# Eight resident Toeplitz tiles, one-hot kernel rows and shared statistics in a decoder layer on one core

## The chip, the cores and the metric

The kernel runs on one core of one Trainium2 chip. The metric is the device time of one execution in microseconds, median of several runs.

## What is computed

One pre-norm decoder layer, all in fp32, on x of 4 sequences x 1024 positions x 256 channels:

```
x = x + mixer(layernorm(x))          # a second layernorm (gamma, beta) inside, then a diagonal
                                     # state-space recurrence over the positions, W_out, b_out,
                                     # and the mixer's own residual
x = x + cross_attention(ctx, ctx, layernorm(x))   # 16 heads, 64 keys a sequence
x = x + ffn(layernorm(x))            # 256 -> 1024 gated, two 1024 x 1024 with gelu, -> 256
h = dA * h + dB * u                  # the recurrence, per channel 64 states
y = sum_n C[n] * h[n] + D * u
```

The recurrence is not stepped. The 1024 positions are cut into 16 chunks of 64. For each channel, what a chunk gives to itself is a 64 x 64 lower triangular Toeplitz matrix (row distance 0 to 63, its entries are the channel's kernel row k[m] = sum over n of w[n] exp(-m alpha[n]), with D added at m = 0), and what it receives from earlier chunks goes through the 64 states.

## The kernel before

The layer is one program for five engines, ordered by hand: each engine has a written list of instructions, and semaphores (`wait_ge`, `then_inc`) tie the lists together. It has two parts. The first, roughly the first 104 us, is the mixer (the functions in `mixer_parts`). Then follow a lead-in for the first block of 512 tokens and a loop over eight such blocks for attention and ffn, in which TensorE is almost always busy. The change touches only the mixer and the places that hand over to it.

The mixer works on these tiles. `xres` holds x by tokens, 32 tiles of 128 tokens x 256 channels. `tok` holds x by channels, 64 columns groups of 128 x 128. `GG` holds for every channel the powers from which kernel rows and carried states are made (128 x 8192). `EE` is the exponent table for the states. `TT` is the Toeplitz matrix of 16 channels (times two halves of the partitions): 128 x 1024 a group, eight groups (`NGRP`) in all.

What each engine does there, in its order:

- **VectorE** (`vector`): coefficients; `GG` by six doublings (`double(0)` to `double(5)`, L337), with token statistics (`stats`, L343 and L346) between them; D added into `GG` at row distance 0 (L397); the rest of the statistics; `variances(b)` and `spreads(b)` for tokens' half b = 0 and 1 (L351 to L363), which give the scales and shifts of the double layernorm; `norms(b)` (L370), which applies them to 12 of the 32 column groups of each half (32 less `ACT_SHARE`); the D entries taken out again (L411); then `gamma(n)` and `beta(n)` (L379, L384) on eight parts of `tok`, of which three must be ready before the first octet; then 16 scans over chunks, one for each octet of channels (L431), with the remaining gammas and betas between them.
- **ScalarE** (`scalar`): exponentials; the decay table (L272); `row_evac(v)` four times (L277): two PSUM banks each of kernel rows into `ksb`; `norm_apply(b)` (L284) on `ACT_SHARE` = 20 of the 32 column groups of each half; the exponentials of `EE` (L289); for each octet the output's evacuation (L304), and the residual base (L292).
- **GpSimd** (`gpsimd_prep`, `gpsimd_core`): constants; inverse square roots by `pow` (L240, L244); `mask(e, g)` for g = 0 to 7 (two affine selects each, L211), which clear the upper triangle of a `TT` tile; `values_clear(0)` (L869); 32 bias sums (L216), of which four stand before mask 7 and the rest behind it.
- **TensorE** (`tensor`): kernel rows by 32 matmuls with a block of ones (L461), in four steps v that each fill two banks; each step writes the same sum to 32 partitions of which one is stored; then `state(0, c)`, and a loop over the octets o = 0 to 16: `state(o + 1)` (L470), `within(o)` (L477, reads `TT`) and `carried(o - 1)` (L484). Octet 0 waits for `z_b` 3 (three betas done); even octets wait for `t_mask`.
- **SyncE** (`sync_mixer`, `sync_core`) issues all transfers in program order: inputs, the kernel rows out to memory (8 stores of 4 rows, L175), then back in as overlapping windows, which makes the Toeplitz tiles (`tt_load`, two transfers a group, L141). `TT` is a ring of four tiles (`TT[g % 4]`), so groups 4 to 7 are loaded in `sync_core` after the octets that use groups 0 to 3 (`w_ps`). Then the ffn weights are copied and loaded, once the last state matmuls are done (`h_ps` 16).

Of the kernel before, what the change touches and what calls it, by code (L numbers as in the profile page):

```python
# [25 lines left out]
F32 = mybir.dt.float32  # L26
# [6 lines left out]
P = 128  # L33
# [21 lines left out]
ACT_SHARE = 20  # L55
# [3 lines left out]
def mixer_parts(nc, ctx, a, t):  # L59
# [7 lines left out]
    def sem(name):  # L67
# [12 lines left out]
    ones = sb("ones", [P, 32], "c")  # L80
# [22 lines left out]
    dtc = sb("dtc", [P, 4], "d")  # L103

    TT = [ring[:, 1024 * k:1024 * (k + 1)] for k in range(4)]
    ksb = ring[:, :].rearrange("p (a m) -> p a m", a=8)
# [7 lines left out]
    kps = [[pair[k][:, 512 * h:512 * (h + 1)] for h in range(2)] for k in (2, 0)]  # L114
# [4 lines left out]
    x_in, E_in, xr_in = ([sem(f"m_{n}{g}") for g in range(8)] for n in ("x_in", "E_in", "xr_in"))  # L119
    const, exps, coef, al_st, coef_t, pk_done, g_row, d_add = (  # L120
        sem("m_" + n) for n in ("const", "exps", "coef", "al_st", "coef_t", "pk_done", "g_row", "d_add"))
    k_ps, k_ev, kr_pad, e_rdy, t_mask = (sem("m_" + n) for n in ("k_ps", "k_ev", "kr_pad", "e_rdy", "t_mask"))
    kr_st = sem("m_kr_st")
    T_in = [sem(f"m_T_in{k}") for k in range(4)]
# [14 lines left out]
    def tt_load(e, g):  # L139
        for h in range(2):  # L140
            e.dma_start(TT[g % 4][L * h:L * h + L, :],  # L141
                        bass.AP(t["kr_h"], (8 * h + g) * (GRP * L), [[1, L], [1, GRP * L]])).then_inc(T_in[g % 4], 16)
# [6 lines left out]
    def sync_mixer(e):  # L149
# [18 lines left out]
        e.dma_start(bo[:, :], a["ab"].partition_broadcast(P)).then_inc(wo_in, 16)  # L168
        e.dma_start(woT[:, :, :], a["aW"]).then_inc(wo_in, 16)
        for v in range(4):  # L170
            for h in range(2):
                u = 2 * v + h
                e.wait_ge(k_ev, u + 1)
                c = (1 - h) * (P * L) + v * 2048
                e.dma_start(kr[0, c:c + 2048].rearrange("(q m) -> q m", q=4), ksb[0:P:32, u, :]).then_inc(kr_st, 16)  # L175
        for n in ("xW", "keys", "scl"):
            e.dma_start(t[n], a[n]).then_inc(k_in, 16)
# [4 lines left out]
        for g in range(2, NGRP):  # L182
            entries_load(e, g)

    def sync_core(e):
        for g in range(4, NGRP):
            e.wait_ge(w_ps, 2 * (g - 4) + 2)
            tt_load(e, g)
# [4 lines left out]
        e.wait_ge(w_d, 48)  # L193
        for n in ("w1", "w2", "w3"):
            e.dma_start(t[n].bitcast(F32), t["d" + n]).then_inc(w_in, 16)
# [10 lines left out]
    def mask(e, g):  # L206
        e.wait_ge(T_in[g % 4], 32 * (g // 4 + 1))
# [10 lines left out]
    def gpsimd_prep(e):  # L218
# [27 lines left out]
        for g in range(1, 4):  # L246
            mask(e, g)
# [1293 lines left out]
```

## Time and profile before

| | |
|---|---|
| median of 3 runs | 929.63 us (928.91 to 930.36) |
| the profiled execution's own time | 931.86 us |
| its span in the profile | 929.9 us |
| busy: PE, PEld, DVE, ACT, POOL | 865.2, 703.3, 524.3, 483.3, 183.7 us |
| mean granted TensorE clock | 0.985 of full |
| first octet's matmuls start | 51.24 us |
| last octet's evacuation starts | 103.56 us |

Times in the profile count from the span's start, in microseconds. PE is TensorE's matmuls, PEld its weight loads, DVE is VectorE, ACT ScalarE, POOL GpSimd, and SPq SyncE's queue of transfers. A matmul call in fp32 leaves two matmul records and two weight load records. In a timeline row the first number is the start, the second the time from the start of the first to the end of the last instruction of the row, then engine, line, operation, what is written and read, and the count; in brackets the idle time of the engine ahead of it and what ended it.

### The profile page before, as it was taken

The numbers are of one execution on the slowest core, as the hardware profiler recorded it, in microseconds if no ns is written. First come the engines' busy times: TensorE is split into PE (matmuls) and PEld (weight loads), VectorE is DVE, ScalarE is ACT, GpSimd is POOL, SyncE is SP. The second block draws the span as 40 slices with busy tenths as digits, with TensorE's granted clock in tenths as the row PEclk, the third lists the DMA queues.
The fourth block names the chain that finished last, engine by engine and source line by source line (L and its number), as shares of the span: only waits on it lengthen the run. The fifth ranks groups of instructions, "written<-read, shape, count | busy, mean of one in ns | idle before, by whom it ended". The sixth has DMA issues, their size and how long they took to land.

```text
span 929.9 us, 15452 instructions
## 1 busy us (share of the span) xinstructions
PE 865.2 (93%) x5762; PEld 703.3 (76%) x5762; DVE 524.3 (56%) x943; ACT 483.3 (52%) x745; POOL 183.7 (20%) x201
## 2 busy tenths in 40 slices
PE   1168999899999999999999999999999999999998
PEld 0067867677887778777877787778777887788887
DVE  7996486465556455555655555464655456464422
ACT  2926543566347634754366536753576256734432
POOL 1567710500031002300130005000500040003000
PEclk9689999999999999999999999999999999999999
DMA  9962698500110002000200010001100110001000
GB/s 341 246 169 50 228 386 344 227 1 1 39 58 0 0 23 73 0 0 0 73 22 0 0 62 34 0 0 51 45 0 0 51 45 0 0 23 45 1 1 25
DMA packets 15641, 61.92 MB, mean 67 GB/s; under 512 B 2851, under 2 KB 4646, under 8 KB 14790
## 3 DMA queue, kind: packets, MB, share of 16 engines
q1 hardware_dynamic: 15574, 61.44, 19.2%
q8 instruction: 24, 0.39, 0.2%
q14 instruction: 11, 0.09, 0.0%
q0 software_dynamic: 32, 0.00, 0.0%
HBM read 49.76 MB, written 23.20 MB: 78 GB/s over the span
## 4 chain that ended last, share of the span: by engine, by line
PE 83%; DVE 9%; issue 5%; ACT 2%; DVEq 0%; POOL 0%; DMA 0%; SPq 0%; POOLq 0%
PE pair L1348 44%; PE pair L1335 9%; PE pair L1360 6%; PE pair L1374 4%; PE pair L1277 4%; PE pair L1288 3%; PE pair L1304 3%; PE pair L470 2%; PE pair L477 2%; PE pair L1297 1%; PE pair L1244 1%; PE pair L484 1%; PE pair L539 1%; DVE vbuf L1150 1%; DVE GG L337 1%
## 5 line engine op out<-in xcount | busy, mean ns | idle before, releaser
L952 ACT ACTIVATE vbuf<-pair,scl 128x512 f32<-128x512 f32 x128 | 87.7, 685 | 231.0 <-PE pair L1348 227.8
L1348 PE MATMUL pair<-h2hi,h_turned 128*128 128x512 f32 x512 | 202.7, 396 | 0.0
L1348 PE MATMUL pair<-h2lo,h_turned 128*128 128x512 f32 x512 | 199.5, 390 | 0.0
L1348 PE MATMUL pair<-h1hi,h_turned 128*128 128x512 f32 x384 | 153.4, 399 | 0.0
L1348 PE MATMUL pair<-h1lo,h_turned 128*128 128x512 f32 x384 | 150.1, 391 | 0.0
L1114 DVE TENSOR_TENSOR h1lo<-vbuf,h1hi 128x512 fp32r<-128x512 f32 x80 | 57.7, 722 | 119.5 <-ACT h1hi L953 118.7
L1348 PEld LDWEIGHTS pair<-h2hi,h_turned 128*128 128x128 f32 x512 | 96.1, 188 | 25.2 <-issue 5.9
L1348 PEld LDWEIGHTS pair<-h2lo,h_turned 128*128 128x128 f32 x512 | 96.2, 188 | 19.3
L1114 DVE TENSOR_TENSOR h2lo<-vbuf,h2hi 128x512 fp32r<-128x512 f32 x64 | 44.3, 692 | 107.0 <-ACT h2hi L953 106.7
L1335 PE MATMUL pair<-zThi,w_turned 128*128 128x512 f32 x224 | 91.7, 410 | 4.1 <-DVE vbuf L1150 4.1
L1348 PEld LDWEIGHTS pair<-h1hi,h_turned 128*128 128x128 f32 x384 | 72.1, 188 | 24.7 <-issue 10.5
L1150 DVE SCALAR_TENSOR_TENSOR vbuf<-pair,scl,sg 128x512 f32<-128x512 f32 x64 | 47.9, 749 | 73.7 <-ACT sg L941 57.5
L1335 PE MATMUL pair<-zTlo,w_turned 128*128 128x512 f32 x224 | 88.8, 396 | 0.0
L845 POOL TENSOR_TENSOR lnv<-lnv 128x4 f32<-128x4 f32 x16 | 16.2, 1015 | 345.2 <-DVE lnv L1019 321.5
L941 ACT ACTIVATE sg<-pair,scl 128x512 f32<-128x512 f32 x64 | 44.1, 688 | 77.6 <-PE pair L1335 67.9
L905 ACT ACT_TABLE_LOAD x65 | 83.4, 1283 | 1.1
L1348 PEld LDWEIGHTS pair<-h1lo,h_turned 128*128 128x128 f32 x384 | 72.2, 188 | 14.2
L877 POOL TENSOR_TENSOR h1lo<-vbuf,h1hi 128x512 fp32r<-128x512 f32 x48 | 61.8, 1287 | 76.7 <-ACT h1hi L944 76.7
L470 PE MATMUL pair<-tok,EE 64*64 64x60 f32 x512 | 38.3, 276 | 26.5 <-DVE tok L384 24.9
L1374 PE MATMUL pair<-w_turned,h1hi 128*128 128x256 f32 x256 | 62.8, 285 | 0.0
L1374 PE MATMUL pair<-w_turned,h1lo 128*128 128x256 f32 x256 | 62.3, 283 | 0.0
L1335 PEld LDWEIGHTS pair<-zThi,w_turned 128*128 128x128 f32 x224 | 42.6, 190 | 20.1 <-DVE vbuf L1150 9.4
(143 smaller groups left out, 1584.5 us busy)
## 6 DMA issues: line engine op xcount, KB each, us to landing
h_turned<-d_h SPq DMA_DIRECT2D x2, 4096.0 KB, 15.0
xres<-in_x SPq DMA_DIRECT2D x8, 512.0 KB, 7.4
tok<-in_xs SPq DMA_DIRECT2D x8, 512.0 KB, 12.2
EE<-alpha_rows SPq DMA_DIRECT2D x16, 256.0 KB, 11.0
ring<-kernel_rows SPq DMA_DIRECT2D x16, 256.0 KB, 4.2
xr<-x_rows SPq DMA_DIRECT2D x8, 512.0 KB, 3.5
out<-xr SPq DMA_DIRECT2D x16, 256.0 KB, 2.0
x_rows<-xres SPq DMA_DIRECT2D x7, 512.0 KB, 12.5
```

The lines of the kernel that those rows point to most:

```text
L470: ins = e.matmul(out, EE[L * h:L * h + L, i, :], rhs, start=True, stop=True)
L877: e.tensor_tensor(h1[1][:, m, :], vb[:, m % 2, :], h1[0][:, m, :], ALU.subtract).then_inc(S["lo"], 1)
L905: e.activation(warm[:, 1:2], warm[:, 0:1], function).then_inc(S["warm"], 1)
L941: e.activation(sg[:, m % 2, :], pair[m % 2][:, 0:512], ACT.Silu, scale=sc1[:, m:m + 1]).then_inc(S["sg_rdy"], 1)
L952: e.activation(vb[:, s % 2, :], h_ps[s % 4], ACT.Gelu, scale=sc)
L1114: e.tensor_tensor(dst[1][:, n % HC, :], vb[:, n % 2, :], dst[0][:, n % HC, :], ALU.subtract).then_inc(S["lo"], 1)
L1150: e.scalar_tensor_tensor(vb[:, m % 2, :], pair[m % 2][:, 512:1024], sc2[:, m:m + 1], sg[:, m % 2, :], ALU.mult, ALU.mult).then_inc(S["v_rd ...
L1277: ins = e.matmul(pair[2][:, g * BLK + b * 256:g * BLK + (b + 1) * 256], qa[64 * g:64 * g + 64, h, tile * P:(tile + 1) * P], kblk[64 * g:64 ...
L1335: ins = e.matmul(pair[m % 2][:, 512 * g:512 * g + 512], w[:, k, m * P:(m + 1) * P], zT[part][:, k * BLK:(k + 1) * BLK], start=(k == 0 and ...
L1348: ins = e.matmul(bank, w[:, k, m * P:(m + 1) * P], src[part][:, k, :], start=(k == 0 and part == 0), stop=(k == HC - 1 and part == 1))
L1360: ins = e.matmul(h_ps[m], h1T[:, k, m * P:(m + 1) * P], h1[part][:, k, :], start=(k == 0 and part == 0), stop=(k == HC - 1 and part == 1))
L1374: ins = e.matmul(pair[2][:, m * DM:(m + 1) * DM], h1[part][:, k, m * P:(m + 1) * P], w3T[:, k, :], start=(k == 0 and part == 0), stop=(k = ...
```

## The change

- `TT` has eight tiles: four in `ring`, four in the space of the ffn weights `w1` and `w2`, which are loaded only later. All eight are loaded in `sync_mixer` and none in `sync_core`. `ksb` moves to the space of `w3`.
- Kernel rows: `ones` becomes `pick`, zeros with one column of ones. `pick[:, 3-v:35-v]` puts the sums of step v on partition 32q + v, and the four steps accumulate in the same two banks. So there is one evacuation of two banks in place of four, placed inside `norm_apply(0)` ahead of its column group `ROWS_AT` = 3. The stores stay eight.
- Statistics of the token tiles 8 to 15 (`ACT_STATS`) move from VectorE to ScalarE (`tile_stats`): a Copy and a Square of each tile with accumulated output, and two small activations for every four tiles.
- `ACT_SHARE` goes from 20 to 18, so VectorE normalises 14 column groups of each half.
- The two reads of the D rows move from VectorE to ScalarE (`w_row`), the two adds and the two restores to GpSimd (`d_add`, `g_back`). Three clears on VectorE move to its start. `norms(1)` moves behind `beta(1)`.
- GpSimd makes its small masks ahead of the Toeplitz masks, starts these only at `z_h` 3 (gamma(2) done), makes all eight in one go, and then does all bias sums; `values_clear(0)` follows them.
- TensorE gets five matmuls without use for the result (128 x 512, `ident` by `GG`) after `z_b` 2, ahead of the first states.
- `bo`, `woT`, `xW`, `keys` and `scl` are transferred after the Toeplitz tiles.

```
-ACT_SHARE = 20
+ACT_SHARE = 18
+ACT_STATS = (8, 16)
+ROWS_AT = 3
...
     def sync_mixer(e):
...
-        e.dma_start(bo[:, :], a["ab"].partition_broadcast(P)).then_inc(wo_in, 16)
-        e.dma_start(woT[:, :, :], a["aW"]).then_inc(wo_in, 16)
-        for v in range(4):
-            for h in range(2):
-                u = 2 * v + h
-                e.wait_ge(k_ev, u + 1)
+        for h in range(2):
+            e.wait_ge(k_ev, h + 1)
+            for v in range(4):
...
         for g in range(4):
             tt_load(e, g)
-        for g in range(2, NGRP):
+            if g in (1, 2):
+                entries_load(e, g + 1)
+        for g in range(4, NGRP):
             entries_load(e, g)
+            if g == 6:
+                e.wait_ge(nat_v, 1)
+            tt_load(e, g)
+        e.dma_start(bo[:, :], a["ab"].partition_broadcast(P)).then_inc(wo_in, 16)
...
     def sync_core(e):
-        for g in range(4, NGRP):
-            e.wait_ge(w_ps, 2 * (g - 4) + 2)
-            tt_load(e, g)
...
     def gpsimd_prep(e):
...
+        e.wait_ge(d_in, 32)
+        e.wait_ge(w_row, 2)
+        e.wait_ge(g_row, 7)
+        for row in (0, N):
+            v = GG[row:row + 1, :, L - 1]
+            e.tensor_tensor(v, v, edit[row:row + 1, 0, :], ALU.add).then_inc(d_add, 1)
+        e.wait_ge(d_add, 2)
+        power(0)
+        e.wait_ge(k_ps, 1)
+        e.wait_ge(powd, 1)
+        for row in (0, N):
+            e.tensor_copy(GG[row:row + 1, :, L - 1], edit[row:row + 1, 1, :]).then_inc(g_back, 1)
+        e.wait_ge(g_back, 2)
+        power(1)
...
+    def gpsimd_core(e):
+        e.wait_ge(z_h, 3)
+        for g in range(NGRP):
             mask(e, g)
-    def gpsimd_core(e):
+        e.wait_ge(t_mask, 2 * NGRP)
         e.wait_ge(wo_in, 32)
...
+        for tile in range(TILES):
+            bias(e, tile)
...
     def scalar(e):
...
+        def tile_stats(first, until):
+            here, n = slice(first, until), until - ACT_STATS[0]
+            e.wait_ge(xr_in[first // 4], 16)
+            if n > 4:
+                e.wait_ge(t_var, n - 4)
+            for j in range(first, until):
+                e.activation(junk[j % 4], xres[:, j, :], ACT.Copy, accum_out=tsum[:, 0, j:j + 1]).then_inc(t_sum, 1)
+            e.wait_ge(t_sum, n)
+            e.activation(tsum[:, 1, here], tsum[:, 0, here], ACT.Copy, scale=-1.0 / (16 * DM)).then_inc(t_mean, 1)
+            e.activation(mvn[:, here, 0], tsum[:, 0, here], ACT.Copy, scale=1.0 / DM).then_inc(t_mean, 1)
+            e.wait_ge(t_mean, n // 2)
+            for j in range(first, until):
+                e.activation(junk[j % 4], xres[:, j, :], ACT.Square, bias=tsum[:, 1, j:j + 1], scale=1.0 / 16, accum_out=mvn[:, j, 1:2]).then_inc(t_var, 1)
...
     def vector(e):
+        for k in range(2):
+            e.memset(hps[k], 0.0).then_inc(h_zero, 1)
+        e.memset(dec[:, :, 0], 0.0).then_inc(dec0, 1)
...
-        stats(4, 8)
+        stats(4, ACT_STATS[0])
+        last_two(0)
         double(5)
...
-        stats(8, 16)
         variances(0)
-        stats(16, 26)
+        stats(SB, SB + 8)
         spreads(0)
-        stats(26, 32)
+        stats(SB + 8, TILES)
+        last_two(1)
         variances(1)
...
         gamma(0)
-        norms(1)
         beta(0)
         gamma(1)
         beta(1)
+        norms(1)
         gamma(2)
         beta(2)
...
     def tensor(e):
...
-                    ins = e.matmul(kps[v % 2][h][32 * q:32 * q + 32, :], ones[N * h:N * h + N, 0:32], GGf[N * h:N * h + N, c:c + 8 * L], start=True, stop=True)
-            ins.then_inc(k_ps, 1)
+                    ins = e.matmul(kps[h][32 * q:32 * q + 32, :], pick[N * h:N * h + N, 3 - v:35 - v], GGf[N * h:N * h + N, c:c + 8 * L], start=(v == 0), stop=(v == 3))
+        ins.then_inc(k_ps, 1)
+        e.wait_ge(pk_done, 7)
+        e.wait_ge(w_row, 2)
+        e.wait_ge(z_b, 2)
+        for _ in range(5):
+            e.matmul(pair[3][:, 0:BLK], ident[:, :], GGf[:, 0:BLK], start=True, stop=True)
...
-        values_clear(0)
         m["gpsimd_core"](e)
+        values_clear(0)
```

## Rows read from the trace of the kernel before

**Rows 1.** Timeline of TensorE, the first octet's state matmuls.

```profile
51.24 1.86 PE L470 MATMUL pair<-tok,EE 64*64 64x60 f32 x30 [24.90 <-DVE tok L384]
```

**Rows 2.** Timeline of VectorE, 0 to 60 us.

```profile
6.00 0.58 DVE L332 COPY edit<-pair 1x128 f32<-1x128 f32 x2
...
19.36 0.84 DVE L397 TENSOR_TENSOR GG<-GG,edit 1x128 f32<-1x128 f32 x2
20.23 0.43 DVE L343 BATCH_NORM_STATS2 stn<-xres 128x6 f32<-128x256 f32 x1
...
31.55 1.02 DVE L406 MEMSET pair<- 128x512 f32 x2
32.49 2.98 DVE L370 TENSOR_SCALAR tok<-tok,spread 128x128 f32<-128x128 f32 x12
...
37.42 1.23 DVE L379 TENSOR_TENSOR tok<-tok,gam 128x1024 f32<-128x1024 f32 x1
38.56 4.95 DVE L370 TENSOR_SCALAR tok<-tok,spread 128x128 f32<-128x128 f32 x12
...
44.56 1.21 DVE L379 TENSOR_TENSOR tok<-tok,gam 128x1024 f32<-128x1024 f32 x1
...
49.14 2.04 DVE L384 TENSOR_TENSOR tok<-tok,bet 128x1024 f32<-128x1024 f32 x1
...
53.28 1.36 DVE L431 TENSOR_TENSOR_SCAN scan<-dec,pair 128x128 f32<-128x128 f32 x4
```

**Rows 3.** Timeline of ScalarE, 0 to 95 us.

```profile
7.09 1.80 ACT L272 ACTIVATE dec<-a 128x1920 f32<-128x1920 f32 x1
...
26.44 1.08 ACT L277 ACTIVATE ring<-pair 128x512 f32<-128x512 f32 x2 [0.24 <-PE pair L461]
28.61 7.80 ACT L284 ACTIVATE tok<-tok,spread 128x128 f32<-128x128 f32 x20 [1.09 <-issue]
...
90.45 2.07 ACT L292 ACTIVATE xres<-xres,ngn,rsn 128x256 f32<-128x256 f32 x4
```

**Rows 4.** Timeline of GpSimd, 20 to 110 us.

```profile
23.92 2.93 POOL L240 TENSOR_TENSOR rn<-sv,mhalf 128x16 f32<-128x16 f32 x1 [20.04 <-DVE sv L354]
...
40.95 5.53 POOL L244 TENSOR_TENSOR rsm<-svn,mhalf 128x32 f32<-128x32 f32 x1
46.55 11.05 POOL L211 TENSOR_SCALAR_AFFINE_SELECT ring<-ring 64x1024 f32<-64x1024 f32 x6
...
89.78 17.25 POOL L216 TENSOR_TENSOR xres<-xres,bo 128x256 f32<-128x256 f32 x25
```

**Rows 5.** Groups by line, 0 to 104 us: busy, mean ns, idle before.

```profile
L461 PE MATMUL pair<-GG,ones 64*32 64x512 f32 x64 | 5.7, 848 | 14.9 <-DVE GG L397 14.6 <-ACT ring L277 0.2
```

**Rows 6.** Timeline of SyncE's queue: stores of kernel rows, first Toeplitz loads.

```profile
23.02 5.04 SPq L175 DMA_DIRECT2D kernel_rows<-ring  x8
...
33.65 4.96 SPq L141 DMA_DIRECT2D ring<-kernel_rows  x8
```

**Rows 7.** Stretches: each engine's busy time, granted clock, DMA share, GB/s.

```profile
40.00:50.00 10.00, 0.00 (x0) 0.00 (x0) 9.93 (x16) 7.34 (x16) 9.78 (x4) 0.50 1.03 238
...
54.00:55.00 1.00, 1.00 (x43) 1.00 (x39) 1.00 (x4) 0.00 (x0) 0.87 (x2) 0.57 1.03 238
...
60.00:70.00 10.00, 9.90 (x361) 9.71 (x358) 8.67 (x18) 5.70 (x9) 3.31 (x4) 1.00 0.40 110
```

**Rows 8.** Chain that ended last: a projection's 16 matmul records, 128x256 each.

```profile
106.47 3.72 PE pair L539 x16
```

**Rows 9.** TensorE's waits, 56 to 103 us: total, times, longest.

```profile
PE pair L477 <- issue: 5.2, 4, 3.0
PE pair L470 <- issue: 1.5, 1, 1.5
```

**Rows 10.** Instruction queue's packets, MB, share: 50 to 60 us, then 60 to 100 us.

```profile
q8 instruction: 1, 0.02, 0.8%
...
q8 instruction: 10, 0.16, 1.8%
```

More of the change, by code:

```diff
@@ L113, in mixer_parts @@
     yps = [pair[k][:, 512 * h:512 * (h + 1)] for k in (2, 0) for h in range(2)]
-    kps = [[pair[k][:, 512 * h:512 * (h + 1)] for h in range(2)] for k in (2, 0)]
+    kps = [pair[2][:, 512 * h:512 * (h + 1)] for h in range(2)]
+    junk = [pair[0][:, DM * k:DM * (k + 1)] for k in range(4)]
     ident = t["ident"]
@@ L193, in sync_core @@
         e.wait_ge(w_d, 48)
+        e.wait_ge(w_ps, NOCT)
         for n in ("w1", "w2", "w3"):
@@ L240, in gpsimd_prep @@
             e.tensor_tensor(rn[:, 0, here], sv[:, here], mhalf[:, 0:SB], ALU.pow).then_inc(powd, 1)
-        mask(e, 0)
-        e.wait_ge(t_mask, 2)
+        e.wait_ge(d_in, 32)
[12 more added lines that the diff above has]
+        power(1)
         e.wait_ge(nat_v, 1)
+        e.wait_ge(powd, 2)
         e.tensor_tensor(rsm[:, :], svn[:, :], mhalf[:, :], ALU.pow).then_inc(natural, 1)
         e.wait_ge(natural, 1)
-        for g in range(1, 4):
+    def gpsimd_core(e):
+        e.wait_ge(z_h, 3)
+        for g in range(NGRP):
             mask(e, g)
-        e.wait_ge(t_mask, 8)
-    def gpsimd_core(e):
+        e.wait_ge(t_mask, 2 * NGRP)
         e.wait_ge(wo_in, 32)
-        done = 0
-        for g, until in ((4, 0), (5, 0), (6, 0), (7, 4), (None, TILES)):
-            for tile in range(done, until):
-                bias(e, tile)
-            done = until
-            if g is not None:
-                e.wait_ge(base_b, done)
-                mask(e, g)
-                e.wait_ge(t_mask, 2 * g + 2)
+        for tile in range(TILES):
+            bias(e, tile)
     def scalar(e):
@@ L272, in scalar, with row_evac @@
         e.activation(dec[:, :, 1:CH], a64[:, :].unsqueeze(2).to_broadcast([P, P, CH - 1]), ACT.Copy).then_inc(dec_rdy, 1)
-        def row_evac(v):
-            e.wait_ge(k_ps, v + 1)
+        e.wait_ge(g_row, 1)
+        for row in (0, N):
+            e.activation(edit[row:row + 1, 1, :], GG[row:row + 1, :, L - 1], ACT.Copy).then_inc(w_row, 1)
+        def tile_stats(first, until):
[11 more added lines that the diff above has]
+                e.activation(junk[j % 4], xres[:, j, :], ACT.Square, bias=tsum[:, 1, j:j + 1], scale=1.0 / 16, accum_out=mvn[:, j, 1:2]).then_inc(t_var, 1)
+        def row_evac():
+            e.wait_ge(k_ps, 1)
             for h in range(2):
-                e.activation(ksb[:, 2 * v + h, :], kps[v % 2][h], ACT.Copy).then_inc(k_ev, 1)
+                e.activation(ksb[:, h, :], kps[h], ACT.Copy).then_inc(k_ev, 1)
         def norm_apply(b):
@@ L292, in residual_base @@
             e.activation(xres[:, j, :], xres[:, j, :], ACT.Identity, bias=ngn[:, j:j + 1], scale=rsn[:, j:j + 1]).then_inc(base, 1)
-        for v in range(4):
-            row_evac(v)
-        e.wait_ge(const, 9)
+        for first in range(*ACT_STATS, 4):
+            tile_stats(first, first + 4)
+        e.wait_ge(const, 10)
         norm_apply(0)
-        entry_exp(0)
         norm_apply(1)
-        for g in range(1, 3):
+        for g in range(3):
             entry_exp(g)
@@ L330, in vector @@
         e.tensor_copy(GG[:, :, L - 1:L], wT.unsqueeze(2)).then_inc(g_row, 1)
-        for row in (0, N):
-            e.tensor_copy(edit[row:row + 1, 1, :], wT[row:row + 1, :]).then_inc(d_add, 1)
         def double(k):
@@ L476, in within @@
                 rows = slice(L * h, L * h + L)
[L477 removed]
+                ins = e.matmul(yps[o % 4][rows, c * BC:(c + 1) * BC], TT[o // 2 % 8][rows, (i % GRP) * PAD:(i % GRP) * PAD + L], tok[rows, :, i], start=(c == 0), stop=False)
             return ins
```

95 lines of the change are left out of this document (48 added, 47 removed).

## The prediction

> **What bounds the kernel now.** I read the chain that ended last first, then the timelines of the five engines to 110 us, then stretches of 10 us, then the queues. Behind the mixer the chain is TensorE itself, and nothing there is edited. In the mixer TensorE has almost nothing to do until the first octet: [rows 1] shows it idle for 24.90 us until the third `beta` ends, and starting at 51.24. So the mixer's front is a chain over VectorE and ScalarE, and what the change is worth is how much earlier that third beta and the first scans come. The reader should follow it in [rows 2] and [rows 3]: doublings to 19.2, D adds, statistics, spreads, norms from 28.61 on ScalarE and from 32.49 on VectorE, gamma(0) at 37.42, the second norms 38.56 to 43.5, beta(2) 49.14 to 51.2, first scan done at 54.64. VectorE has no idle time of note in it. In [rows 7] VectorE is busy 9.93 of 10 us in the stretch from 40.
>
> From the first octet on, TensorE sets the pace: [rows 7], second row, has 361 matmul records in 9.90 us, 27.4 ns each, so an octet of 96 records takes 2.6 us. The ring of four Toeplitz tiles does not hold it: TensorE's waits from 56 to 103 us are 5.2 and 1.5 us of "issue" [rows 9], none on a mask. So eight resident tiles by themselves save nothing there; what they give is freedom in placing GpSimd's masks.
>
> **The sum, step by step.** Before-times stand in the rows, after-times are worked out.
>
> 1. The two D reads leave VectorE (0.58 from 6.00), two aggregates (0.2 together) come ahead of `double(5)`: it ended just ahead of the adds at 19.36, at 19.2 [rows 2], so now at 19.2 - 0.5 + 0.2 = 18.9. The three clears that left (two are the 1.02 at 31.55) now lie at VectorE's very start, where it waits for its first inputs, and cost nothing; without that cover about 1.2.
>
> 2. D adds on GpSimd. The trace has no such add there. VectorE's are 0.42 each [rows 2]; above, a 128x256 bias sum on GpSimd is 0.69 (17.25/25) [rows 4]; below I go to 0.2. I take 0.45, as one row of 128 elements is nearer to VectorE's row: done at 19.85, +-0.5.
>
> 3. Kernel rows on TensorE: the same 64 records, busy 5.7 [rows 5], now without waits for evacuations: 19.9 to 25.7.
>
> 4. Statistics on ScalarE. It is free when the decay table is done, 7.09 + 1.80 = 8.9 [rows 3]; two D reads of 0.2 follow. A 128x256 activation with two pointer operands is paced at 0.52 (2.07/4) [rows 3]; 16 of them are 8.3, four small ones at 0.2 and their waits 1.1, so 18.7 without any price for the accumulated output. For that the trace has nothing. Bounds: a gain, since Copy has no pointer operands and may be faster (-2), and a further small activation each (+0.2 each, +3.2). I take +1: done at 19.7. Nothing is queued on ScalarE meanwhile that anyone needs (its row evacuations came from 22.4 on). Who waits is `variances(0)` on VectorE, free at 18.9, and behind it `power(0)` on GpSimd, free at 19.85. So up to 19.8 this is nearly free, then each microsecond counts fully.
>
> 5. `power(0)` 2.93 [rows 4]: 19.9 to 22.8. VectorE makes eight statistics meanwhile (pace 0.39, 20.23 onward [rows 2]), 3.1, also done near 23. Spreads take 1.0, about what ScalarE idled ahead of 28.61 [rows 3]: ready at 23.9, against 28.5 before. 4.6 us gained, from eight tiles fewer (3.1) and ten fewer statistics behind the first `variances`, up to where the pow ends last.
>
> 6. ScalarE: three column groups (0.39 each, 7.80/20), then the evacuation, for which `k_ps` comes at 25.7, ends 26.8 (1.08 for two banks), then 15 groups: 32.6 [rows 3]. Without `k_ps` in time this end moves with it. VectorE: eight statistics 3.1, small ones 0.5: 27.5; 14 norms at 0.244 (2.98 for 12 [rows 2], beside a pow on GpSimd): 30.9. `power(1)`: GpSimd copies D back after 25.7 (0.9), then 27.4 to 30.3, hidden. Spreads(1) until 31.9. The copies and the clear that stood ahead of gamma(0) are gone too. gamma(0) starts at 32.7, bound by ScalarE with 0.8 to spare on VectorE; before 37.42.
>
> 7. Two gammas and two betas at 1.15 (44.56 and its successor [rows 2], beside the long pow): 37.3. `norms(1)`, 14 groups: 3.4 at the undisturbed pace; before, it took 4.9 for 12 because masks began at 38.27 beside it [rows 2]. The bound above is that pace, 5.8. GpSimd now runs only the long pow and tiny masks here: 3.4, to 40.7. ScalarE's second half, 32.6 + 18 x 0.39 = 39.6, is hidden. gamma(2) 1.15: 41.9. Then the masks start, and beta(2) runs beside them: 2.04 as at 49.14: 43.9, against 51.2. gamma(3) likewise: 46.0; first scan 46.0 to 47.3, against 54.64: 7.3 gained.
>
> 8. TensorE. The five useless matmuls are 10 records of 128x512. A 128x256 record is 0.23 at the high clock [rows 8], so 0.47, and 0.93 at the low one. The granted clock is 0.50 (1.2 GHz) over 40 to 50 [rows 7]; in the trace it rose within the stretch 54 to 55 (mean 0.57), some 3.6 us after the first octet began, and is 1.00 at 60. With the same delay from 37.3: four records slow, six fast, 6.5 us, done at 43.8, just as beta(2) ends. Bounds: never fast, 46.6; still under the scan's 47.3 for the states alone, costing about 1. The first octet then runs at 2.4 GHz; before, it ran at 1.2 GHz up to there. Mask 0 is two selects at 1.84 (11.05/6 beside gammas [rows 4]): 45.6, then 64 records, 47.4. So octet 1's carried part starts at about 47.4, against 55.4: 8.0 gained.
>
> 9. Transfers. The row stores start at 26.3 in place of 23.02 and issue for 5.0 [rows 6], to 31.4; before, the last ended at 28.06 and the first load was issued at 33.65, behind a full queue. With `bo`, `woT` and three more moved behind, I expect 2.5 for the last landing: loads from 34, tile 0 at about 38, needed at 41.9. Even the old 5.6 leaves a microsecond or so. Later tiles: 512 KB a group for each of `TT` and `EE` at 238 GB/s [rows 7] is 4.4 us a pair; tile 7 lands near 65. Masks go on at 1.84 a select to about 70, group g done at 45.6 + 3.7g, needed at about 5.7g + 45; in time. `bo` is in by 68, bias sums 70 to 94 at 0.69; before they ended at 107. The ffn weights are triggered by the last states and so shift along.
>
> 10. Inside the loop: while masks run, VectorE's gamma or beta is 2.04 in place of 1.2, with a 1.3 scan 3.35 per octet against TensorE's 2.6. The lag grows 0.6 to 0.7 an octet, has about 1.3 of slack, and TensorE's own stalls give more back: I charge 0.5. And 0.5 for stalls in code fetch beside transfers that now last to 65 and not to 58.
>
> Sum: 8.0 - 0.5 - 0.5 = 7.0. The profiled execution had 931.86 with a span of 929.9, so 924.9 and 922.9; the median of the runs is 2.2 below the former: **922.6 us**. Differences below 0.2% (1.9 us) I count as no change.
>
> **A rule that speaks against it.** In [rows 2] four gammas and betas keep their 1.15 beside GpSimd's 5.53 us pow (40.95 to 46.5 [rows 4]). 
> - *The lock moves into the loop.* If select and gamma alternate worse than 2.04, VectorE becomes the pace for eight octets: 0.75 each less the slack, 8 x 0.75 - 1.3 - 1.5 = 3.2: 925.3. Against: scans beside masks keep 1.36 [rows 2].
> - *Code fetch beside transfers; this is the way to slower.* TensorE's longest stall, 3.0 us [rows 9], came with the only instruction block that its queue (q8) fetched in the stretch with full DMA engines; ten more follow in the 40 us behind 60 [rows 10], mostly with idle DMA engines, and with them only 2.2 + 1.5 us of stalls [rows 9]. After the change, at one block in 4 us from 47 to 65, five or so fall into the full stretch. Each that shows costs up to 3.0: one or two, 925.6; four, 12 us less what overlaps VectorE's lag, about 930 to 932. From three it eats the gain. For: one of one was exposed. Against: its excess over the other stalls is only 1.5. The Trainium skill (Runtime: NRT & Kernel Launch, "Instruction fetch mechanics") calls crossing a block mostly hidden; the 3.0 disagrees.
> - *The long pow does block gammas*: gamma(0) at 35.8, 3.1 lost: 925.7.
> - *Hidden anyway*: something behind the mixer with a time of its own (ffn weights, `keys`) takes up the gain: no change, 929. Against: all of it is triggered by mixer steps that move too.
>
> **Chances.** Forecast 0.65 (own range 920.7 to 924.5: GpSimd's adds +-0.5, accumulation -0 to +1.5, lag 0 to 1, fetch 0 to 1). Dear accumulation 0.12, lock in the loop 0.07, fetch 0.12 (half of it still faster, 0.02 no change, 0.04 slower), pow 0.02, hidden 0.02. Faster 0.65 + 0.12 + 0.07 + 0.06 + 0.02 = 0.92, same 0.04, slower 0.04. The range takes in the three cases near 925 and leaves out the fetch case's tail: 920.7 to 926.3.
>
> **What would show it.** Right: spreads(0) copied near 23; gamma(0) near 32.7; `norms(1)` 3.4 for 14; first states near 44; first scan near 46; granted clock 1.00 there; no wait on masks in the loop; last evacuation near 96.5 and everything behind shifted alike. Wrong: VectorE idle before `variances(0)` on ScalarE's Square; extra instructions after each accumulating one; TensorE "issue" waits in the loop well above 5.2 + 1.5 in total; TensorE waiting for scans; mask 0 waiting for its load.

## The result

The changed kernel takes **932.48 us** (median of 10 executions, 931.24 to 934.33), the kernel before, run beside it, 930.10. The ratio is 1.0024, 95% interval 1.0014 to 1.0033: slower by 0.24%, where 922.6 us was forecast. The profiled execution is 934.33 us, the slowest of the ten, with a span of 932.6, 2.7 us above the span before.

Up to the first scan everything came as forecast. ScalarE's timeline (start, duration, engine, line; the accumulated output shows as an instruction of its own) answers to step 4:

```profile
15.30 0.36 ACT L303 ACTIVATE pair<-xres 128x256 f32<-128x256 f32 x1
15.61 0.18 ACT L303 ACTIVATION_READ_ACCUMULATOR pair<-xres 128x1 f32 x1
...
17.65 0.46 ACT L309 ACTIVATE pair<-xres,tsum 128x256 f32<-128x256 f32 x1
18.05 0.19 ACT L309 ACTIVATION_READ_ACCUMULATOR pair<-xres,tsum 128x1 f32 x1
```

GpSimd's timeline, answering to [rows 4]: D adds, first power, long power, the masks, the last 20 bias sums.

```profile
19.26 1.14 POOL L258 TENSOR_TENSOR GG<-GG,edit 1x128 f32<-1x128 f32 x2 [15.21 <-DVE GG L377]
20.48 2.94 POOL L252 TENSOR_TENSOR rn<-sv,mhalf 128x16 f32<-128x16 f32 x1
...
31.33 5.53 POOL L269 TENSOR_TENSOR rsm<-svn,mhalf 128x32 f32<-128x32 f32 x1
...
42.77 13.40 POOL L221 TENSOR_SCALAR_AFFINE_SELECT ring<-ring 64x1024 f32<-64x1024 f32 x8 [4.22 <-issue]
...
89.17 13.84 POOL L226 TENSOR_TENSOR xres<-xres,bo 128x256 f32<-128x256 f32 x20 [1.86 <-ACT xres L331]
```

VectorE's timeline, answering to [rows 2]: gamma(0), norms(1), gamma(2), beta(2), gamma(3), first scan.

```profile
32.85 1.22 DVE L425 TENSOR_TENSOR tok<-tok,gam 128x1024 f32<-128x1024 f32 x1 [0.17 <-issue]
...
37.65 3.67 DVE L416 TENSOR_SCALAR tok<-tok,spread 128x128 f32<-128x128 f32 x14
41.42 1.23 DVE L425 TENSOR_TENSOR tok<-tok,gam 128x1024 f32<-128x1024 f32 x1
42.69 1.23 DVE L430 TENSOR_TENSOR tok<-tok,bet 128x1024 f32<-128x1024 f32 x1
43.83 2.17 DVE L425 TENSOR_TENSOR tok<-tok,gam 128x1024 f32<-128x1024 f32 x1
45.92 1.34 DVE L466 TENSOR_TENSOR_SCAN scan<-dec,pair 128x128 f32<-128x128 f32 x4
```

The first scan starts at 45.92 (46.0 forecast, 53.28 before): 7.4 us gained. At TensorE it is less. Its first matmul of the carried part (47.4 forecast) stands in its timeline at 49.39:

```profile
49.39 0.32 PE L522 MATMUL pair<-scan,GG 64*64 64x64 f32 x2
```

And in the same view of the kernel before:

```profile
55.41 0.26 PE L484 MATMUL pair<-scan,GG 64*64 64x64 f32 x2
```

That is 6.0 us gained and not 8.0. TensorE's timeline of the changed kernel shows the wait for mask 0 and then three holes:

```profile
47.05 0.30 PE L508 MATMUL pair<-tok,EE 64*64 64x60 f32 x2 [1.23 <-POOL ring L221]
...
52.99 0.27 PE L522 MATMUL pair<-scan,GG 64*64 64x64 f32 x2 [2.43 <-issue]
...
61.81 0.37 PE L515 MATMUL pair<-tok,ring 64*64 64x64 f32 x2 [5.06 <-issue]
...
70.54 0.27 PE L515 MATMUL pair<-tok,ring 64*64 64x64 f32 x1 [4.41 <-issue]
```

"Issue" means that nothing in the trace was waited for; 2.43 + 5.06 + 4.41 = 11.9 us. The stretches, answering to [rows 7] (PE's busy time comes first after the length; then, at the end, the granted clock, DMA share, GB/s):

```profile
50.00:60.00 10.00, 4.32 (x142) 3.91 (x139) 6.43 (x10) 1.64 (x2) 9.07 (x8) 0.94 1.04 229
60.00:70.00 10.00, 4.32 (x127) 4.09 (x127) 5.23 (x10) 3.21 (x5) 6.32 (x6) 0.74 1.04 251
70.00:80.00 10.00, 9.46 (x314) 9.46 (x314) 6.01 (x13) 4.94 (x9) 6.04 (x7) 0.75 0.15 34
```

In 20 us TensorE makes 142 + 127 records, where [rows 7] has 361 in ten. The DMA engines are full up to 70 (shares of 0.87 and 0.40 in these stretches before), and behind each of the two long holes TensorE runs at 1.2 GHz again: stretches of 1 us at 63, 71 and 74 are granted 0.50, the one at 75 is at 0.98. TensorE's instruction blocks come on their own queue, q8; its packets in 50 to 60, 60 to 70 and 70 to 80 us:

```profile
q8 instruction: 2, 0.03, 1.7%
...
q8 instruction: 1, 0.02, 0.9%
...
q8 instruction: 3, 0.05, 2.1%
```

Before, 60 to 70 had three. Narrow windows of the same view give each packet's place: in the changed kernel they start at 50.13, 58.97 and 67.72 (the expectation of the first experiment has these 0.2 us late) and take 1.3 to 1.4 us each, and the three holes end at 52.99, 61.81 and 70.54, each 2.8 to 2.9 us behind the start of its packet. Once under way a block is hardly slower than elsewhere (0.9 to 1.4 us behind 70); what is late is its start. In the kernel before, the 3.0 us hole ends 2.7 us behind the packet of 56.92. A smaller one, 1.5 us, ends 2.45 us behind the packet of 69.81, with a DMA share of only 0.26 from 70 to 80, so not every exposed block had full DMA engines beside it. The evacuation of the last octet, from ScalarE's timeline of the changed kernel:

```profile
104.38 0.60 ACT L342 ACTIVATE tok<-pair 128x512 f32<-128x512 f32 x1 [0.57 <-PE pair L522]
```

And the same view of the kernel before:

```profile
103.56 0.60 ACT L304 ACTIVATE tok<-pair 128x512 f32<-128x512 f32 x1 [0.57 <-PE pair L484]
```

So between the first scan and the last evacuation the 7.4 us are lost, and 0.8 more. Of these 8.2, 5.9 are added waits at issue (12.6 in place of 6.7) and 1.2 the wait for mask 0. The other 1.9 us of the span's 2.7 come behind the mixer, where nothing is edited: in the stretches from 165 to 175 the granted clock is lower than before. The changed kernel's:

```profile
165.00:170.00 5.00, 2.12 (x6) 1.67 (x6) 3.56 (x7) 1.32 (x2) 1.27 (x1) 0.72 0.26 107
170.00:175.00 5.00, 5.00 (x18) 3.96 (x17) 0.75 (x1) 1.47 (x3) 1.28 (x1) 0.60 0.86 315
```

The same stretches of the kernel before:

```profile
165.00:170.00 5.00, 2.87 (x8) 2.24 (x9) 2.74 (x4) 0.63 (x1) 1.28 (x1) 0.75 0.26 105
170.00:175.00 5.00, 5.00 (x26) 4.15 (x25) 1.50 (x2) 2.41 (x4) 2.30 (x2) 0.91 1.09 413
```

### The profile page after: what moved, and what is told of

The parts are those of the page before. It is cut to its first block, busy times and chain, and to the rows that moved or that the text cites. A ratio compares the mean times of both kernels' runs of the same rounds, so it can differ in the third digit from the quotient of the medians.

```text
span 932.6 us, 15491 instructions
## 1 busy us (share of the span) xinstructions
PE 872.9 (94%) x5772; PEld 708.6 (76%) x5772; DVE 519.1 (56%) x925; ACT 487.9 (52%) x773; POOL 186.0 (20%) x206
## 4 chain that ended last, share of the span: by engine, by line
PE 83%; DVE 7%; issue 6%; ACT 2%; POOL 1%; DVEq 0%; DMA 0%; SPq 0%; POOLq 0%
PE pair L1386 44%; PE pair L1373 9%; PE pair L1398 6%; PE pair L1412 4%; PE pair L1315 4%; PE pair L1326 3%; PE pair L1342 3%; PE pair L508 2%; PE pair L515 2%; PE pair L1335 1%; PE pair L1282 1%; PE pair L522 1%; PE pair L577 1%; DVE vbuf L1188 1%; DVE GG L377 1%
## 5 line engine op out<-in xcount | busy, mean ns | idle before, releaser
L1152 DVE TENSOR_TENSOR h2lo<-vbuf,h2hi 128x512 fp32r<-128x512 f32 x64 | 44.2, 691 | 107.0 <-ACT h2hi L991 106.7
L1386 PEld LDWEIGHTS pair<-h1hi,h_turned 128*128 128x128 f32 x384 | 72.1, 188 | 24.7 <-issue 10.5
L897 POOL TENSOR_TENSOR kblk<-keys,hmask 128x256 f32<-128x256 f32 x18 | 10.7, 613 | 208.0 <-PE pair L1315 207.9
```

Of the source, the lines that this page charges most:

```text
L1152: e.tensor_tensor(dst[1][:, n % HC, :], vb[:, n % 2, :], dst[0][:, n % HC, :], ALU.subtract).then_inc(S["lo"], 1)
L1386: ins = e.matmul(bank, w[:, k, m * P:(m + 1) * P], src[part][:, k, :], start=(k == 0 and part == 0), stop=(k == HC - 1 and part == 1))
```

## The experiments

Theory F: with 16 full DMA engines TensorE's next instruction block comes late, and the change brings TensorE into that stretch. Rivals: L, GpSimd's selects and VectorE's operations hold each other up; A, the load on the transfers doesn't matter. Later came theory G: what the mixer gains is given back where the next phase waits for bias sums. All results in one table. "Issue" is TensorE's waits of that kind from 30 to 106 us, "last" the start of the last octet's evacuation, both from the profiled execution. The ratios are to the kernel before on the same chip, whose medians were 930.63 (e1 to e4), 930.23 (e5 to e8), 931.55 (e9 to e11) and 930.62 (e12). Where the text compares two runs in microseconds, these are differences of medians, and the kernel before alone moved by 1.45 from one set to another; the ratios are the safer comparison.

| run | us | ratio, 95% interval | issue | last |
|---|---|---|---|---|
| before | 930.10 | 1 | 6.7 | 103.56 |
| after | 932.48 | 1.0024 (1.0014, 1.0033) | 12.6 | 104.38 |
| e1_late | 930.30 | 0.9999 (0.9988, 1.0010) | 10.2 | 102.22 |
| e2_traffic | 935.27 | 1.0061 (1.0046, 1.0075) | 10.5 | 108.10 |
| e3_wide | 1039.33 | 1.1179 (1.1161, 1.1198) | 0.0 | 203.17 |
| e4_small_masks | 930.72 | 1.0010 (1.0000, 1.0020) | 12.4 | 103.62 |
| e5_paced | 932.24 | 1.0024 (1.0009, 1.0040) | 1.3 | 95.06 |
| e6_fill | 930.23 | 1.0008 (0.9995, 1.0021) | 9.6 | 102.66 |
| e7_fill_paced | 927.11 | 0.9967 (0.9953, 0.9981) | 3.8 | 94.99 |
| e8_fill_late | 928.74 | 0.9983 (0.9971, 0.9994) | 8.6 | 100.97 |
| e9_fill_spread | 924.37 | 0.9930 (0.9912, 0.9949) | 4.3 | 96.54 |
| e10_before_paced | 934.23 | 1.0037 (1.0022, 1.0052) | 0.3 | 107.83 |
| e11_paced_spread | 927.87 | 0.9969 (0.9957, 0.9982) | 3.0 | 97.3 |
| e12_before_eased | 932.48 | 1.0027 (1.0015, 1.0040) | 5.8 | 103.12 |

**Tiles 4 to 7 loaded late**, in the changed kernel:

```diff
     def sync_core(e):
+        for g in range(4, NGRP):
+            e.wait_ge(w_ps, 2 * (g - 4) + 2)
+            if g == 6:
+                e.wait_ge(nat_v, 1)
+            tt_load(e, g)
```

> The changed kernel with its eight tiles, but groups 4 to 7 loaded as in the kernel before: each only after the octets that use group g - 4. Theory F (TensorE's code blocks are fetched late while the queues are full of transfers): in the changed kernel the blocks came 8.8 us apart (50.35, 59.19, 67.95) with the DMA engines full to about 71 us, and 3.6 us apart later. Here 2 MB less are queued, so the full stretch ends near 60: the stall at 66 goes (4.4 us), the one at 57 stays or shrinks; 926 to 929. Rival L (GpSimd's masks beside VectorE's gammas set the octets' pace): masks 0 to 3 are as dense as before, so the time stays within 1 us of the changed kernel, 931.5 to 933.

2.2 us came back, in the last evacuation and in the median alike; the waits at issue fell only from 12.6 to 10.2. The time, 930.30, lies outside both ranges, between them. Fewer transfers in the stretch help, but two holes of the three stay (2.0 and 4.5 us), and the third is down to 1.1. The profiled execution gained more, 5.2 us of span: 3.0 of them behind the mixer, where its clock is granted 1.00 from 165 to 175 (0.72 and 0.60 in the changed kernel).

**Useless loads in the kernel before**, 2 MB behind the exponent groups:

```diff
         for g in range(2, NGRP):
             entries_load(e, g)
+        for g in range(4):
+            for h in range(2):
+                e.dma_start(more[...], ...).then_inc(more_in, 16)
...
```

> The kernel before with eight more transfers of 256 KB each, that nothing needs, queued behind the exponent tables (into space that is free until the ffn weights come). Nothing else changes. Theory F: the full stretch goes from 58.5 to about 67; the blocks that came at 60.7 and 64.4 come about 6 us late each, so TensorE's issue waits grow from 6.7 to 11 to 16 us, and the time from 930 to 934 to 938. Rival L, and the rival that the stalls come from the order of the instructions and not from transfers: no change, 930.

Nothing reads these loads in the mixer, and yet it lost 4.5 us there and 4.6 in the time, as F said; the waits at issue grew to 10.5, just under the 11 to 16 expected. Its stretches 50 to 70:

```profile
50.00:60.00 10.00, 6.31 (x182) 6.08 (x184) 9.04 (x14) 0.00 (x0) 8.97 (x11) 0.67 1.04 244
60.00:70.00 10.00, 6.85 (x197) 6.66 (x193) 4.83 (x10) 2.23 (x3) 0.40 (x2) 0.67 1.02 225
```

From 50 to 70 q8 brought TensorE two blocks, where the kernel before had four. One hole of 3.1 us ends at 67.15, and GpSimd has almost no work from 60 to 70 here, so it is not the selects. F stands, A falls.

**One transfer a group instead of two**, through a source of three dimensions:

> The changed kernel with each Toeplitz tile and each exponent group loaded by one transfer to 128 partitions in place of two to 64 partitions each (same bytes). The two-part loads move 238 GB/s, the token loads to 128 partitions 410 GB/s. Theory F with this: if the one-part loads run near 400 GB/s, 7.3 MB take 18 us from 33 and end near 52 in place of 65, and the blocks from 59 on are not late: 924 to 926. If they keep 238 GB/s, no change from the changed kernel. Rival L: no change either way, 932.5.

A miss that tests nothing of F: with loads under way all the time, about two of the 16 DMA engines were busy (12.1% of 16 is 1.9). Its queue from 35 to 80 us (packets, MB, share of the 16 engines) moved 2.15 MB in 45 us, and TensorE waited 30.4 us for tiles up to 106.

```profile
q1 hardware_dynamic: 579, 2.15, 12.1%
```

**Selects cut to one channel of 16**, so that 15 of the 16 matrices of each tile stay unmasked (a part of the computation is left out):

```diff
-            v = TT[g][L * h:L * h + L, :].rearrange("p (d t) -> p d t", d=GRP)
+            v = TT[g][L * h:L * h + L, 0:L].rearrange("p (d t) -> p d t", d=1)
-                            pattern=[[0, GRP], [-1, L]], ...
+                            pattern=[[0, 1], [-1, L]], ...
```

> The changed kernel with the affine selects cut to one of the 16 channels of each tile, so 15 of 16 Toeplitz matrices keep entries above the diagonal (that part of the computation is left out). All transfers stay. Theory F: the stalls stay (12 us of issue waits), only beta(2), gamma(3) and the first mask are faster by some 2 us ahead of them, and that is lost again in the first late block: 931 to 933. Rival L: VectorE's gammas go back to 1.2 us, the octets run at TensorE's pace, 924 to 926.

The waits at issue stay (12.4), in three holes of 3.9 to 4.1 us, though VectorE's gamma beside the masks is back at 1.26. L, which needed 924 to 926, falls as the cause of the holes. The time, 930.72, is just under F's range: without the selects the mixer ends 0.8 us earlier, and by the ratios the kernel gains 1.3.

**Loads paced**: the second half of each load waits until the load before it has landed, so at most three are under way.

```diff
+    def paced(e, items):
+        past = None
+        for kind, g in items:
+            for h in range(2):
+                if past is not None and h == 1:
+                    e.wait_ge(past[0], past[1] + 32)
+                if kind == "T" and g == 6 and h == 0:
+                    e.wait_ge(nat_v, 1)
+                (tt_load if kind == "T" else entries_load)(e, g, (h,))
+            past = (xr_T_in[g], 16) if kind == "T" else (E_in[g], 0)
```

> The changed kernel, same loads in the same order, but SyncE issues the second half of each load only when the load before it has landed, so at most three transfers (768 KB) are under way in place of up to 3 MB. Theory F1 (a code block waits behind what is queued ahead of it in the DMA engines): the blocks in the loop come 4 to 6 us apart in place of 8.8, the issue waits fall from 12.6 to 4 to 7 us, 925 to 929. Theory F2 (a code block is slow because the DMA engines are busy, whatever is queued): the same total of transfers, perhaps stretched, so the stalls stay or get more: 931 to 936.

The stretch from 50 to 60 of this run:

```profile
50.00:60.00 10.00, 9.20 (x328) 8.86 (x324) 10.00 (x18) 3.70 (x5) 6.12 (x5) 0.95 0.55 159
```

And its q8 packets in the same 10 us:

```profile
q8 instruction: 3, 0.05, 1.9%
```

The packets of q8 now start at 51.04, 56.15, 59.95, 63.47 and 67.01, and the holes are gone: the waits at issue are 1.3, where F1 had 4 to 7 and F2 no less than before. The last evacuation starts 9.3 us earlier than in the changed kernel, yet the time is the same and lies in the range of F2. So the time does not decide, the waits do: the gain of the mixer is lost behind it, as shown below. F1 (a block waits behind what is queued) and F2 (a block is late because the engines are busy) are not told apart by this run, as pacing took down both: the share fell from 1.04 to 0.55. TensorE's waits behind the mixer, 92 to 180 us (total, times, longest), in this run:

```profile
PE pair L1292 <- DVE nat L1067: 7.2, 2, 6.6
```

And in the changed kernel:

```profile
PE pair L1289 <- DVE nat L1064: 0.6, 1, 0.6
```

Tile 7 was masked only at 84.6, and all 32 bias sums, which stand behind it in GpSimd's list, ran from 88.3 to 110.3. VectorE's first sums of the next phase, which theory G names, were done by 102.8. What TensorE waited for is the normalised tile `nat`, and `nat` waits for an inverse root on GpSimd (`lnv`) that stands in its list behind the bias sums. VectorE's timeline of this run:

```profile
103.80 6.50 DVE L1078 TENSOR_SCALAR lnv<-mv 128x4 f32<-128x4 f32 x1
113.06 1.38 DVE L1067 TENSOR_SCALAR nat<-xres,mv,lnv 128x256 f32<-128x256 f32 x4 [2.77 <-POOL lnv L886]
```

And GpSimd's:

```profile
112.01 1.02 POOL L886 TENSOR_TENSOR lnv<-lnv 128x4 f32<-128x4 f32 x1
```

In the changed kernel GpSimd starts this root at 113.36 and VectorE the tile at 114.42, so of the 9.3 us 1.4 are left here. (VectorE's own small operation in the first row takes 0.17 there; here it took 6.50 and ended at 110.30, with the last bias sum. Why it was held is not shown.) TensorE, idle ahead of `nat`, was then granted 0.50 from 110 to 118, where the changed kernel has 1.00, and at VectorE's `lead_prob` (120.52 against 120.69) 0.2 are left. So nearly all of the 9.3 is placed: 7.9 us went at GpSimd's order, 1.2 more by 120.7, in and behind the stretch at 1.2 GHz.

**Exponent groups 2 to 4 loaded ahead of the kernel rows' stores**, with three orders of the rest: at once, paced, and with tiles 4 to 7 late as in the first run.

> The changed kernel with the exponent groups 2 to 4 issued right behind groups 0 and 1, in the 7 us in which the DMA engines have little to do (30 to 37), and not between the Toeplitz tiles. All else is queued as in the changed kernel. F1 and F2 alike: the full stretch ends some 5 us earlier (66), so of the three late blocks the third is on time: 4 us less, 927 to 930. If the Toeplitz tiles come too late for mask 0 (needed at 42.8), TensorE waits for POOL ahead of the loop and 1 to 3 us are lost.

> Both: exponent groups 2 to 4 early, the rest paced as in e5. F1: issue waits below 5 us and the whole gain of the mixer's front (7 us) left over: 922 to 926. F2: like e6 or worse, 928 to 932.

> Exponent groups 2 to 4 early, group 5 behind Toeplitz tile 3, and tile 4 to 7 with exponent groups 6 and 7 only as the octets pass (as the kernel before did for the tiles). The queues are short from 50 us on, with bursts of 2.2 to 4.4 us. F1 and F2: issue waits of 4 to 7 us as in the kernel before, the front's 7 us are kept: 922 to 926. Rival (late loads hold the masks up behind each other, and the bias sums behind them): TensorE or VectorE waits on POOL, 927 or more.

Moving loads into the idle queue ahead takes 2.2 us off the changed kernel (1.5 by the ratios, whose intervals overlap). With pacing as well, 5.4; again TensorE waited for VectorE behind the mixer (4.0 in place of 0.6), and the bias sums ran from 85.1 to 107.0. All three came out slower than F had said: 930.23 for 927 to 930, 927.11 for 922 to 926, 928.74 for 922 to 926. In the third the waits at issue were 8.6 for 4 to 7, and TensorE waited only 0.9 for a mask, so its rival, late masks, doesn't explain it.

**Bias sums between the masks**, on top of the paced run with early groups, and of the plain paced one; `bo` and `woT` are loaded behind tile 3.

```diff
         for g in range(NGRP):
             mask(e, g)
-        e.wait_ge(t_mask, 2 * NGRP)
-        e.wait_ge(wo_in, 32)
-        for tile in range(TILES):
+            e.wait_ge(t_mask, 2 * g + 2)
+            if g == 4:
+                e.wait_ge(wo_in, 32)
+            if g in (4, 5):
+                for tile in range(6 * (g - 4), 6 * (g - 3)):
+                    bias(e, tile)
+        for tile in range(12, TILES):
             bias(e, tile)
```

> The kernel with groups 2 to 4 of the exponent rows loaded early and the later loads paced (927.11 us) brought the mixer's last evacuation to 94.99, 9.4 us ahead of the changed kernel, and only about 5 us of it reached the end. Theory G (given back at the bias sums): its 32 bias sums ran in one go behind mask 7, 85.1 to 107.0, and TensorE waited 4.0 us for VectorE's first sums of the next phase, which need them. Here bias and output matrix are loaded behind tile 3, and twelve bias sums run in GpSimd's own waits for tiles (six behind mask 4, six behind mask 5). G: the bias sums end near 99, the last evacuation stays at 95 to 96, TensorE's 4.0 us of waits for VectorE there go, and the time is 922 to 924.5 us. Rival R (something else behind the mixer sets the start of the next phase: the weights, or the clock after it): bias sums end near 99 as well, and the time stays at 926 to 928.

> The changed kernel with paced loads (932.24 us, last evacuation 95.06) and the same interleaving of twelve bias sums with the masks as in the run above, bias and output matrix loaded behind tile 3. In that kernel the bias sums ran from 88.3 to 110.3 and TensorE waited 7.2 us for VectorE's first sums of the next phase. Theory G: those 7.2 us go nearly whole, bias sums end near 102, and the time is 925 to 927 us. Rival R (another thing sets the start of the next phase): 930 to 932 us.

G holds in that the end of the bias sums sets the start of the next phase, by way of `lnv` as above. GpSimd's timeline of the first of the two:

```profile
68.06 7.01 POOL L231 TENSOR_TENSOR xres<-xres,bo 128x256 f32<-128x256 f32 x6
...
87.88 13.79 POOL L231 TENSOR_TENSOR xres<-xres,bo 128x256 f32<-128x256 f32 x20
```

And TensorE's waits of that run, for the same operand as above:

```profile
PE pair L1298 <- DVE nat L1073: 0.6, 1, 0.6
```

The wait for VectorE is back at 0.6, the last evacuation starts at 96.54, 7.8 us ahead of the changed kernel's, and 8.1 us arrive at the end: **924.37 us, the fastest here, 0.7% below the kernel before.** Two of its numbers missed: the bias sums end at 101.7 (99 expected), and the last evacuation starts 1.55 us later than in its parent, as tile 7 is masked 3.4 us later (85.4). In the other run 4.4 us arrive over its paced parent, and 927.87 is 0.9 above what I had expected. There tile 7 is masked at 87.8, 3.2 us later than in the parent, TensorE waits 0.9 for tiles and 3.4 for ScalarE (2.6 in the parent), and the last evacuation starts 2.2 us later; the clock between 95 and 105 is granted at 0.92 and 0.74, against 1.00, which I leave unexplained.

**The same cure in the kernel before**, in two forms:

> The kernel before with its ten loads of tiles 0 to 3 and of exponent groups 2 to 7 paced as in the runs before this one, and nothing else changed. Theory F (TensorE's instruction blocks arrive late beside queued transfers) says that the kernel before pays for it too: its stalls between 56 and 70, some 5 us with the clock at half behind the longest, shrink to under 2 us, its last evacuation comes at 100 to 101.5 in place of 103.56, and the time is 926.5 to 928.5 us; that much of the gain of the paced kernels isn't the change's. Rival (the kernel before had its stalls beside transfers that it can't do without, or the later exponent groups come too late when paced): 929.5 to 931 us.

> The run before paced all ten loads of the kernel before and came out slower, because tiles 4 to 7 stood on the same queue behind the paced exponent groups (their issue went from 60.6 to 74.1 and TensorE waited 11.5 us for mask 4), though its waits at issue fell from 5.2 to 0.3 us. Here only tiles 0 to 3 and groups 2 to 4 are paced, group 5 is loaded ahead of tile 4, and groups 6 and 7 behind tiles 4 and 5. Theory F: the stalls stay under 2 us, mask 4 starts by 66 as before, the last evacuation comes at 100 to 101.5 and the time is 926.5 to 928.5 us: the kernel before pays about 3 us for late instruction blocks too, and the change with its own cure (924.37 us) is worth some 3 us over that. Rival (the change's earlier start is worth all of the difference, and the kernel before gains nothing from pacing): 929.5 to 931.5 us. Rival (pacing is all there is to it, and the change brings nothing): 924 to 925.5 us.

Two misses. In the first, the queue's waits for pacing stood ahead of the loads of tiles 4 to 7, and TensorE waited for the mask of tile 4, as its waits from 30 to 106 us show:

```profile
PE pair L476 <- POOL ring L217: 11.5, 1, 11.5
PE pair L490 <- issue: 0.3, 1, 0.3
```

The stalls at issue did go (0.3 against 6.7), as F says, but the design hid what that is worth. In the second they did not go (5.8, where under 2 was expected), mask 4 started at 71.3 (65.3 before) and the last evacuation only 0.4 earlier; its median is still 1.9 us above the kernel before, which its trace, of an execution of 931.75, does not explain. Its four-tile ring lets tiles 4 to 7 load only as earlier ones come free, so they met the later exponent groups in the same stretch. In neither form did pacing help the kernel before; an order of its loads that does may exist and wasn't found.

## Why the prediction was wrong

- **Steps 1 to 7 were right**, to 0.1 us in their sum (first scan 45.92 for 46.0). Single terms moved against each other. GpSimd's D adds take 0.57 each, not 0.45. The statistics end at 18.2, not 19.7: an accumulated output adds an instruction of 0.18 to 0.20, of which 0.09 shows in the pace (0.40 for Copy, 0.49 for Square). norms(1) took 3.67, not 3.4. beta(2) kept 1.23, since it had begun (42.69) just ahead of the masks (42.77), and gamma(3), beside them, took 2.17.
- **Step 8 failed by 2.0 us.** It gained 8.0 at the first matmul of the carried part, the figure that the sum starts from; measured are 6.0 (49.39 for 47.4, against 55.41). The five matmuls did what they should: 6.04 us for 6.5, and the clock at 1.00 from 44 to 46. But mask 0 began at 42.77 for 41.9 and released TensorE at 47.05 for 45.6, so TensorE waited 1.2 us; the clock fell to 0.50 behind that wait (stretches of 1 us at 48, 49 and 50); and from 47.05 to the carried part took 2.3 us, where the step had 1.8 for 64 records (the same stretch took 2.6 in the kernel before, 52.81 to 55.41).
- **Step 9** placed the transfers well: loads issued from 33.1 (34 forecast), mask 0 not held by its load, tile 7 masked at 68.7. What it left out is that each microsecond by which TensorE starts earlier, with the stores later, is a microsecond more of TensorE beside full DMA engines.
- **Step 10 failed**, and this is the larger part, at its last term: "0.5 for stalls in code fetch beside transfers". Measured are 12.6 us of waits at issue in place of 6.7, so 5.9 where the term had 0.5, and the low clock behind them. From the carried part on 6.8 us were lost (6.0 gained there, -0.8 at the last evacuation), and 5.9 of them are this. The rival "code fetch beside transfers" named the place, the queue and the size: three holes, 11.9 us, where it had 3.0 each and four for about 930 to 932. It got a chance of 0.12 because [rows 9] and [rows 10] held one exposed block in a full stretch, 3.0 us long, beside smaller ones elsewhere. That one block was one of one: the only sample in the state into which the change moves five, and I weighed it as an outlier. A sum in which every block in the full stretch costs its 3.0 would have been slower than before.
- The other charge of that step, 0.5 for VectorE's lag, can't be read from the changed kernel, whose holes give VectorE time to catch up. In the paced run TensorE waited 0.7 us for a scan, once, and VectorE was busy all 20 us from 50 to 70. The last evacuation there starts at 95.06, ahead of the forecast's 96.5, but with 5.4 us less of issue waits than the sum had kept from the kernel before; so with the stalls gone something else in the loop (VectorE's lag, or the 1.8 us that TensorE waited there for ScalarE) costs more than 0.5. How it divides is not shown.
- **"Everything behind shifted alike"** held for 924.37 us, but not by itself: with the mixer 9.3 us shorter, the end of GpSimd's bias sums became what the next phase waits for. In the changed kernel they end at 103.0 (94 forecast, though 32 at its 0.69 from 70 on give 92), as ScalarE's bases, which they add to, come between the late octets.
- Rivals: dear accumulation and the blocking pow did not happen (gamma and beta kept 1.22 each beside the pow of 31.33 to 36.86; the prediction counts four beside the same pow before, its rows' timeline has three, from 43.43). The lock in the loop stayed near its forecast, 2.16 for 2.04. "Hidden anyway" was not what the changed kernel met, but it came true in part for the paced ones, by GpSimd's list. The runs whose bias sums were not in the way gained in the median about what the last evacuation of their trace gained (e1 2.2 for 2.2, e6 2.2 for 1.7, e8 3.7 for 3.4, e9 8.1 for 7.8); how close the pairs are is in part luck, since the clock behind 165 differs between these traces.
- Open: that clock. It is granted below 1.00 somewhere from 165 to 175 in the traces of the kernel before, the changed one, e4, e5, e8, e10 and e12, and at 1.00 throughout in e1, e2, e6, e7, e9 and e11; between the changed kernel and e1 or e6 some 3 us of span hang on what lies behind the mixer, as much as several of the effects above. No run was made for it. Open too is how the DMA engines share between q8 and the loads: that many queued loads, with the engines full, delay a block's start is shown; whether by the queue or by the busy engines is not.

## What to carry to other kernels

Before an engine is moved to start earlier, look at what the DMA engines do in the stretch into which it moves: a long unrolled instruction stream needs its own transfers, and one exposed block in the old trace is a better first price for each of the new ones than nothing (3.0 us there, 2.4 to 5.1 here). Spread or pace bulk loads that are not urgent so that few are queued at once, but never with waits that stand ahead of an urgent load on the same queue. And when a phase gets shorter, list what ran under its cover (here the bias sums), and what stands behind that on the same engine: if it ends no earlier than it did, it takes the gain.

## What the runs showed of the hardware

- With the DMA engines full (share 1.04, 229 and 251 GB/s), q8 brought TensorE three blocks in 20 us (50 to 70), and five in the same 20 us with the loads paced (share 0.55 and 0.54, 159 and 160 GB/s). The holes were 2.4 to 5.1 us, and each ended 2.8 to 2.9 us behind the start of a packet that itself took 1.3 to 1.4. The Trainium skill (Runtime: NRT & Kernel Launch, "Instruction fetch mechanics") calls crossing a block mostly hidden; beside queued loads these runs disagree.
- After the holes of 5.1 and 4.4 us TensorE ran again at 1.2 GHz for 3.0 and 4.5 us before 2.4 GHz was granted. It made 32 and 31 records a microsecond there (62 to 65, 71 to 75), and 39 from 75 to 79 at 2.4 GHz: an estimate from these rows is 1.5 us on top of the two holes. From 48 to 50, also at 1.2 GHz, it made 40, so the level alone does not set the pace.
- Pacing gave up rate (159 in place of 229 GB/s), and TensorE waited no longer for masks in the paced run than in the changed kernel (1.2 us). What the late masks cost, as far as its trace shows, is what stood behind them on GpSimd.
- Loads merged so that the source's outermost dimension is 2 kept about 2 of the 16 DMA engines busy, 12.1% in the row above.
